# DLRM tower: the last shift's 39 field pairs as one matmul of rounded parts, and the diagonals on ScalarE

## The reference

```
for W in (f0, f1, f2):                       # f0 (39*39, 128); f1, f2 (128*39, 128)
    z = einsum('bfd,bgd->bfgd', x0, xk).reshape(b, f * g, d)
    cur = einsum('bpd,pm->bmd', z, W)        # 128 maps for each sample and each d
    outs.append(cur); xk = cur
z = sum over d of concatenate(outs, axis=1)  # (512, 384)
h = relu(concatenate([z, dense_ctx]) @ W_top1 + b_top1)
h = relu(h @ W_top2 + b_top2)
y = h @ W_top3
```

## Time and profile before

| what | value |
|---|---|
| median of 3 runs | 661.05 us (660.89 to 661.32) |
| profiled execution | 660.73 us, its span 658.5 us |
| busy in the span | PE 625.5, VectorE 522.7, GpSimd 502.3, ScalarE 341.3 us |
| mean granted TensorE clock | 0.99 |
| first strip matmul of chunk 0 | 42.41 us |
| first matmul of the dense layers that close the kernel (L893) | 628.47 us |

### The profile page before, as it was taken

The page is one execution under the profiler, slowest core; times in us unless marked ns, Lnnn a source line. Parts: engine busy times, 40 slices in busy tenths (PEclk is TensorE's granted clock), DMA queues, the critical chain, the costliest instruction groups (busy, mean ns, idle before and its releaser), DMA issues.

```text
span 658.5 us, 10966 instructions
## 1 busy us (share of the span) xinstructions
PE 625.5 (95%) x3110; PEld 470.4 (71%) x3110; DVE 522.7 (79%) x1655; ACT 341.3 (52%) x1152; POOL 502.3 (76%) x486
## 2 busy tenths in 40 slices
PE   0559999999999999999999999999999999999998
PEld 0237777777788777777788777777788777778873
DVE  4239988989985888989984888989984889988911
ACT  3224555646463565646463564646463564646612
POOL 6717888989894889989894888989894897657620
PEclk9969999999999999999999999999999999999999
DMA  7423405641320404031220404131230403000000
GB/s 226 106 57 111 127 3 134 236 105 32 68 68 2 132 3 121 15 90 47 60 75 3 131 4 110 25 92 44 52 84 2 131 4 104 27 1 2 0 1 0
DMA packets 59014, 43.40 MB, mean 66 GB/s; under 512 B 37648, under 2 KB 42926, under 8 KB 58826
## 3 DMA queue, kind: packets, MB, share of 16 engines
q1 hardware_dynamic: 52334, 37.52, 19.6%
q0 software_dynamic: 5120, 1.32, 2.9%
q10 hardware_dynamic: 1500, 3.87, 1.7%
HBM read 40.75 MB, written 1.94 MB: 65 GB/s over the span
## 4 chain that ended last, share of the span: by engine, by line
PE 91%; another core or an unknown queue 3%; DVE 2%; DMA 2%; ACT 1%; issue 1%; ACTq 1%; DVEq 0%
PE strip L816 22%; PE strip L820 22%; PE strip L817 22%; PE acc L776 14%; PE acc L847 4%; PE strip L834 3%; PE strip L847 1%; DVE scaled L593 1%; DMA g_sum<-in_L_rec_f 1%; PE strip L918 1%; PE acc L785 1%; ACT w_hi L717 1%; ACTq L720 1%; PE strip L896 0%
## 5 line engine op out<-in xcount | busy, mean ns | idle before, releaser
L593 DVE SCALAR_TENSOR_TENSOR scaled<-strip,x_t,scaled 128x128 f32<-128x128 f32 x1216 | 331.5, 340 | 31.0 <-PE strip L820 29.5
L816 PE MATMUL strip<-w_hi,x_hi 128*128 128x512 f32 (+1 forms) x640 | 297.0, 464 | 3.4 <-ACT x_hi L646 3.4
L820 PE MATMUL strip<-w_hi,x_lo 128*128 128x512 f32 (+1 forms) x640 | 249.4, 390 | 0.0
L817 PE MATMUL strip<-w_lo,x_hi 128*128 128x512 f32 (+1 forms) x640 | 248.8, 389 | 0.0
L488 POOL TENSOR_TENSOR added<-added,product 128x512 f32<-128x512 f32 x128 | 173.0, 1351 | 83.4 <-ACT product L702 76.9
L702 ACT ACTIVATE product<-strip,x_t 128x128 f32<-128x128 f32 x512 | 147.0, 373 | 126.5 <-PE strip L820 113.2
L478 POOL DMA_INDIRECT found<-in_tables,rows x160 | 159.6, 998 | 28.4 <-issue 11.2
L816 PEld LDWEIGHTS strip<-w_hi,x_hi 128*128 128x128 f32 x640 | 120.5, 188 | 52.5 <-issue 18.8
L817 PEld LDWEIGHTS strip<-w_lo,x_hi 128*128 128x128 f32 x640 | 120.8, 189 | 45.5 <-issue 25.3
L820 PEld LDWEIGHTS strip<-w_hi,x_lo 128*128 128x128 f32 x640 | 120.3, 188 | 25.8
L776 PE MATMUL acc<-z,w 117*128 117x512 f32 (+1 forms) x238 | 116.5, 572 | 9.1 <-issue 9.1
(11 more groups left out here) (57 smaller groups left out, 190.2 us busy)
## 6 DMA issues: line engine op xcount, KB each, us to landing
shifted<-x_fields SPq DMA_DIRECT2D x105, 234.0 KB
x_thrice<-x_fields SPq DMA_DIRECT2D x15, 234.0 KB
found<-in_tables,rows POOLq DMA_INDIRECT x160
w<-in_L_rec_f SPq DMA_DIRECT2D x1, 2496.0 KB, 11.9
g_sum<-in_L_rec_f ACTq DMA_DIRECT2D x4, 512.0 KB
shifted<-x_half_fields SPq DMA_DIRECT2D x10, 117.0 KB
x_once<-x_fields SPq DMA_DIRECT2D x15, 78.0 KB
x_fields<-found SPq DMA_DIRECT2D x15, 72.0 KB
```

What stands on the lines that cost most here:

```text
L593: dve.scalar_tensor_tensor(into, strip[:, slot_of_strip(q) % Y_BANKS, j, :], x0_t[:, c % 2, s, f:f + 1], onto, ALU.mult, ALU.add).then_inc ...
L816: pe.matmul(into, x1_hi[:, c % 2, columns], hi, start=True, stop=False)
L817: pe.matmul(into, x1_hi[:, c % 2, columns], lo, start=False, stop=False)
L820: pe.matmul(into, x1_lo[:, c % 2, columns], hi, start=False, stop=True).then_inc(strip_ready, 1)
```

## The change

For parts 3 to 16 (`STACKED_FROM = 3`) the seventh tile goes away. The pairs of shift 18 move into the eleven unused partitions (117 to 127) of tiles 2 to 5, in runs of eleven pairs, which need their own field ranges beside `x0_thrice` and `shifted` and, for tiles 4 and 5, a second copy `x0_thrice2`. The pairs of shift 19 are computed as a product `z0_last` in which each pair stands on three neighbouring rows. ScalarE rounds it to `z0_last_hi`; VectorE combines both with `roles` into `z0_stack`, whose three rows hold the rounded part, the rounded part and the rest (with a sign). The weights are made once in the same way (`w0_stack`: rounded, rest, rounded). One f32r matmul adds the three products to `acc0`. The products start at place 9 instead of 6, the matmuls at 15 instead of 12, the stacked one is at place 33. The diagonals are made by ScalarE in two activations with `mask` as the scale.

```
+STACKED_FROM = HALVES + 1
+FULL = T0 - 1
+EXTRA = P - ROWS
+EXTRA_FROM = FULL - 4
+EXTRA_PAIRS = [(EXTRA_FROM + k, k // 2 * EXTRA, k // 2 * EXTRA + (LAST_SHIFT - 1 if k % 2 == 0 else FIELDS - LAST_SHIFT + 1))
+               for k in range(4)]
-PRODUCT0_AT = [6, 9, 12, 15, 18, 21, 24]
-LAYER0_AT = [12, 15, 18, 21, 24, 27, 30]
+PRODUCT0_AT = [9, 12, 15, 18, 21, 24]
+LAYER0_AT = [15, 18, 21, 24, 27, 30, 33]
-PRODUCT0_LATE_AT = [10, 13, 16, 19, 22, 25, 28]
-LAYER0_LATE_AT = [16, 19, 22, 25, 28, 31, 34]
+PRODUCT0_LATE_AT = [11, 14, 17, 20, 23, 26]
+LAYER0_LATE_AT = [17, 20, 23, 26, 29, 32, 34]
+STACK_AT = (6, 17, 27)
+STACK_LATE_AT = (8, 18, 29)
+W0_STACK_AT = (1, 23)
...
+                at_least(sp, z0_last_ready, i - 1 - STACKED_FROM)
+                sp.dma_start(x0_thrice[0:ROWS, p, columns_of(i)], shifted_fields(i, 0, PER_TILE, 0)
                              ).then_inc(thrice_in[p], 16)
+                if i >= STACKED_FROM:
+                    sp.dma_start(x0_thrice[ROWS:P, p, :], some_fields(i, EXTRA_PAIRS[0][1])).then_inc(thrice_in[p], 16)
                 if i:
                     once(i)
+                if i >= STACKED_FROM:
+                    at_least(sp, z0_last_ready, i - STACKED_FROM)
+                    sp.dma_start(shifted_last[:], shifted_fields(i, LAST_SHIFT, PER_TILE, 0)
+                                 ).then_inc(shifted_last_in, 16)
+                for t in range(tiles_of(i) if i else T0_BY_SP):
+                    at_least(sp, z0_ready, pairs_before(i - 1) + t + 1 if i else 0)
+                    if i >= STACKED_FROM and t == EXTRA_PAIRS[2][0]:
+                        sp.dma_start(x0_thrice2[0:ROWS, p, :], shifted_fields(i, 0, PER_TILE, 0)
+                                     ).then_inc(thrice2_in[p], 16)
+                        sp.dma_start(x0_thrice2[ROWS:P, p, :], some_fields(i, EXTRA_PAIRS[2][1])
+                                     ).then_inc(thrice2_in[p], 16)
+                    if rows_of(i, t) == P:
+                        sp.dma_start(shifted[ROWS:P, t, :], some_fields(i, EXTRA_PAIRS[t - EXTRA_FROM][2])
+                                     ).then_inc(shifted_in[t], 16)
...
+            def products_last(i):
+                dve.wait_ge(thrice_in[p], 16 * (arrivals(i) + stacked_arrivals(i)))
+                dve.wait_ge(shifted_last_in, 16 * (k + 1))
+                at_least(dve, z0_stack_ready, k)
+                dve.tensor_tensor(z0_last[:], shifted_last[:], x0_thrice[0:ROWS, p, :], ALU.mult
+                                  ).then_inc(z0_last_ready, 1)
+            def stack(i):
+                dve.wait_ge(z0_last_ready, k + 1)
+                dve.wait_ge(z0_last_hi_ready, k + 1)
+                if k:
+                    dve.wait_ge(l0_step, T0 * i)
+                dve.scalar_tensor_tensor(z0_stack[:], z0_last[:], roles[:, 0:1], z0_last_hi[:].bitcast(F32),
+                                         ALU.mult, ALU.subtract).then_inc(z0_stack_ready, 1)
...
+            def high_last(i):
+                act.wait_ge(z0_last_ready, k + 1)
+                at_least(act, z0_stack_ready, k)
+                act.copy(z0_last_hi[:], z0_last[:]).then_inc(z0_last_hi_ready, 1)
+            def diagonal(c):
+                act.wait_ge(x0_t_ready, part_of(c, SUBS - 1) + 1)
+                act.wait_ge(mask_in, 16)
+                at_least(act, g_ready, c)
+                for b in range(TILE_B):
+                    last = act.activation(x0_diag[:, :, b, 0:FIELDS], x0_t[:, c % 2, :, :], ACT.Copy,
+                                          scale=mask[:, b:b + 1])
+                last.then_inc(diag_ready, 1)
...
+                if t == tiles_of(i):
+                    pe.wait_ge(z0_stack_ready, i - STACKED_FROM + 1)
+                    if i == STACKED_FROM:
+                        pe.wait_ge(w0_stack_ready, 1)
+                    pe.matmul(acc0[:], w0_stack[:], z0_stack[:], start=False, stop=True).then_inc(l0_step, 1)
+                    return
```

More of the change, by code:

```diff
@@ L71, in columns_of, with pairs_before, tiles_of, step_of_product @@
     return slice(HALF_N * i, HALF_N * i + HALF_N) if i < HALVES else slice(0, N)
+def pairs_before(i):
+    return T0 * min(i, STACKED_FROM) + FULL * max(i - STACKED_FROM, 0)
+def tiles_of(i):
+    return T0 if i < STACKED_FROM else FULL
+def step_of_product(m):
+    i = max(i for i in range(X0_PARTS) if pairs_before(i) <= m)
+    return T0 * i + m - pairs_before(i) + 1
+def rows_of(i, t):
+    return P if i >= STACKED_FROM and t >= EXTRA_FROM else ROWS
+def transfers_of(i, t):
+    return i + 1 + (max(i + 1 - STACKED_FROM, 0) if EXTRA_FROM <= t < FULL else 0)
+def stacked_arrivals(i):
+    return len(range(i, STACKED_FROM - 1, -2))
 def subs_of(i):
@@ L287, in build_program @@
         shifted_in = [sem(f"shifted_in_{t}") for t in range(T0)]
+        thrice2_in = [sem(f"thrice2_in_{k}") for k in range(2)]
+        shifted_last_in = sem("shifted_last_in")
+        w0_last_in = sem("w0_last_in")
+        roles_in = sem("roles_in")
+        w0_last_ready = sem("w0_last_ready")
+        w0_last_hi_ready = sem("w0_last_hi_ready")
+        w0_last_lo_ready = sem("w0_last_lo_ready")
+        w0_signed_ready = sem("w0_signed_ready")
+        w0_stack_ready = sem("w0_stack_ready")
+        z0_last_ready = sem("z0_last_ready")
+        z0_last_hi_ready = sem("z0_last_hi_ready")
+        z0_stack_ready = sem("z0_stack_ready")
         w0_ready = sem("w0_ready")
@@ L926, in _, with pair_rows @@
             last.then_inc(y_done, 1)
-def shift_rows():
-    upper = np.full((ROWS, T0), -1)
-    lower = np.full((ROWS, T0), -1)
+def pair_rows():
+    upper = np.full((P, T0), -1)
+    lower = np.full((P, T0), -1)
+    last_upper = np.full((ROWS, 1), -1)
+    last_lower = np.full((ROWS, 1), -1)
     for s in range(SHIFTS):
@@ L938, in shift_rows @@
                 lower[row, t] = h * FIELDS + g
-    return upper, lower
+    taken = set()
+    for t, begin, partner in EXTRA_PAIRS:
+        for k in range(EXTRA):
+            g, h = (begin + k) % FIELDS, (partner + k) % FIELDS
+            if frozenset((g, h)) not in taken:
+                taken.add(frozenset((g, h)))
+                upper[ROWS + k, t] = g * FIELDS + h
+                lower[ROWS + k, t] = h * FIELDS + g
+    assert taken == {frozenset((g, (g + LAST_SHIFT - 1) % FIELDS)) for g in range(FIELDS)}
+    for g in range(FIELDS):
+        h = (g + LAST_SHIFT) % FIELDS
+        last_upper[PER_TILE * g:PER_TILE * g + PER_TILE] = g * FIELDS + h
+        last_lower[PER_TILE * g:PER_TILE * g + PER_TILE] = h * FIELDS + g
+    return upper, lower, last_upper, last_lower
 def by_gathers(of_fields, at_once):
```

110 lines of the change are left out of this document (81 added, 29 removed).

## The result

The median went from 661.18 us (660.89 to 661.75, 4 runs) to 657.01 us (656.18 to 657.51, 4 runs): ratio 0.9934, 95% interval [0.9913, 0.9954]. So the change is faster, by 4.2 us or 0.7%, where 9.7 us were forecast (651.4, range 650.3 to 655.0). The profiled execution took 657.29 us, its span 655.7 (2.8 less than before).

A forecast was written before the change was run, and what follows sets the result against it. The prediction took PE's instruction stream to set the time from 42 us on. From 660.73 us, -8.8 (PE) and -0.9 (stall) gave 651.0, or 651.4 for the median; own range 650.4 to 653.6, widened to 650.3 to 655.0.

The forecast's parts named there:

- GpSimd paragraph: GpSimd does the same work, its waits for ScalarE shrink by 1.3 us in all, some 0.4 us stays; cost nothing.
- Eight such operations stay eight: VectorE's two-SBUF-operand operations, which don't overlap GpSimd additions, stay eight a chunk since the diagonal leaves.
- PE: In 14 stacked parts one f32 tile (0.86 us) gives way to one 0.233 us matmul: 8.8 us saved.
- upper bound of the matmul: Stacked matmul on PE: 0.44 us if its weight load stands in front (0.19 more), against 0.233 taken.
- The stall of the earlier trace: PE's late weight load for strip 7's bank: excess 1.5 us, all gone at most, none at least, 0.9 taken.
- VectorE: Stacking (0.89 us) replaces the diagonal (0.93): net nothing per chunk, bounds -0.25 to +1.2, covered by 2.12 us idle.
- the sign named: Sign of being right: VectorE's idle before strip 31 still above 1 us.
- weight operations of chunk 1: Once-only rounding of weights at place 23, about 1.3 us of VectorE, before its 2.12 us idle: nothing.
- ScalarE: Two diagonal activations and one rounding copy add 1.6 us a chunk and fit; nothing, at worst 0.5 us of VectorE's time.
- Transfers: About +19% bytes and added issues end some 5 us later, at the turn of the chunk; cost nothing.
- A: Rival: shifted GpSimd collisions, late banks at strips 10 to 14 or a showing load cost 0.2 to 0.5 us in 14 chunks: 654 to 658; chance 0.12.
- D: Rival: GpSimd holds the chunk at 35, needing 0.5 us more work to hold at 34.5, 1.1 for no gain; chance 0.02.

The follow-up runs named there:

- e1: Changed kernel with gathers (GpSimd's indirect field loads) moved out of ordinary chunks into chunk 0 and layer-2 chunks: 647.19 against 646.62 us for the kernel before, 1.001.
- e9: Changed kernel with no gather (GpSimd's indirect field load) in the last quarter of a chunk: 641.19 against 646.53 us for the kernel before, 0.9922.
- e2: Kernel before the change with the same dealing of gathers as e1: 656.75 us, 1.0164 of the kernel before.
- e10: Kernel before the change with the same dealing as e9, no gather in the last quarter of a chunk: 647.21 us, 1.0012 of the kernel before.
- e11: Kernel before the change with only the diagonals moved from VectorE to ScalarE: 647.14 us, 1.0005 of the kernel before.
- e14: Changed kernel as it is, the base on one chip with the early start: 640.07 us, 0.9887 of the kernel before.
- e16: e3 again, changed kernel without the stacking operation, on the same chip as e14: 638.81 us, 0.9877 of the kernel before.
- e3: Changed kernel with VectorE's stacking operation left out, the matmul reading z0_last_hi: 639.10 against 646.62 us for the kernel before, 0.9885.
- e12: Kernel before the change with tiles three places later and diagonals on ScalarE, all seven f32 tiles kept: 645.15 us, 0.9981 of the kernel before.
- e4: Kernel before the change with the seventh tile's matmul cut to 16 columns from part 3 on: 638.71 against 646.62 us, 0.9886.
- e17: Changed kernel with 22 gathers for 26 ahead of the loop and gathers dealt anew, ordinary chunks none in the last quarter: 649.25 against 660.74 us before, 0.9829.
- e7: Changed kernel with the diagonal back on VectorE as one operation at place 20: 669.41 against 661.29 us for the kernel before, 1.0112.
- e18: Changed kernel as it is, the base on the same chip as e17: 656.16 us, 0.9933 of the kernel before.
- e8: Kernel before the change with only its ordinary tile places moved three later: 665.21 us, 1.0058 of the kernel before.
- e13: As e9, changed kernel, with 22 gathers for 26 ahead of the loop and first chunks dealt anew: 638.36 against 646.95 us for the kernel before, 0.9868.

## Why the prediction was wrong

**Step that failed: the GpSimd paragraph.** "It does the same work", "it keeps some 0.4 us", "Cost: nothing". The same instructions took 32.6 to 33.1 us in the saturated chunks instead of 31.4. With gaps between instructions of 2.5 us that is 35.1, over the 34.32 that PE needs. Before, gaps and waits were 3.8 us, so 1.3 were waits. With those waits the 1.4 us that collisions with two-operand operations added a chunk cost nothing, and the prediction took the waits for free room and put no price on collisions on GpSimd's side. Chunks 1 to 14 gained 4.9 us of the forecast 9.7; the other 4.8 are lost here. It is shown by e1 and e9 (lighter or moved GpSimd work frees the chunks) with e2 and e10 as the control, and by PE's waits for L600.

**"Eight such operations stay eight"** was the count, and it misled. A collision is worth what stands on the other side: the diagonal left a place where it had cost GpSimd 0.1 us (e11), and the stacking came to one where it begins inside an addition and pushes the next gather (0.3 us; e14 to e16: 0.3 to 0.5 us in three of the four chunks). The larger part is not the stacking: e3, without it, still has GpSimd at 31.8 to 32.1. By the trace, the six products and the last one lengthen GpSimd's operations by 2.7 us in chunk 7, where seven products did so by 1.3 in chunk 6 before. What moved them against GpSimd's operations, the new places or PE's shorter chunk, no run separates; e12 has the places without the rise (30.9 to 31.5 us in the ordinary chunks 2 to 11), and e4 has the relief alone, with the rise in one chunk.

**PE: right.** Strips stand 0.93 us apart around place 33, the matmul costs 0.233. 34.94 (e12) to 34.32 is 0.62 us where 0.627 was forecast. Had all chunks run so, chunks 1 to 14 would take 11 x 34.32 + 3 x 43.01 = 506.6 and the time would be 5.0 less, of which 1.2 is chunk 2, 0.8 each of the other four saturated ones, 0.1 each of the layer-2 chunks and 0.2 chunk 6. The upper bound of the matmul, 0.44, would by its own terms be 0.233 + 0.19 = 0.42, and the range's lower end, 650.4, lacks the 0.3 us that the forecast adds for the median; neither bears on the miss.

**The stall of the earlier trace rows: right in effect, wrong in the reason.** Of the chunks that had it, 14 lost it (35.06 to 34.32) and 6 kept 0.17 of its 0.24 us; in the five saturated ones the wait for `x2_t` stands in its place. Where GpSimd's work is dealt out otherwise, it is gone from all (34.32 in e9 from chunk 3 on), so there the upper end, 1.5 us, held rather than 0.9. But e12 loses it without any PE relief, from places and diagonals alone; it does not need the 0.23 us behind strip 31.

**VectorE: too low a price, little harm.** The stacking took 1.12 us where 0.89 was taken, and the 91 products of 512 columns average 1045 ns, where 885 was read (the last product: 783). VectorE's work rose from 32.76 to 33.55 us in a saturated chunk, inside the bound of +1.2. Idle before strip 31 fell to 0.15 us in chunk 7, where over 1 was the sign named. It holds PE for 0.2 us between strips 20 and 21 of each saturated chunk, which is gone where GpSimd's work is lighter (e1, e9), and for over 1 us in chunk 2 of e9 and e17. There the weight operations of chunk 1, priced at nothing because an idle of 2.12 us would follow, found no such idle.

**ScalarE: right.** Two diagonals of 439 ns and a cast of 634: 1.5 us where 1.6 was forecast, and its work in a chunk rose by 1.1. That the move pays only together with the places was not in the prediction: e7 puts its absence at 12.7 us, e11 its presence alone at nothing.

**Start: the clock in chunk 0, the rest not settled.** The first strip was 1.0 us later and chunk 0 0.9 longer. The stretch of chunk 0 in the changed kernel had a mean granted clock of 0.93 of the higher level (2.4 GHz); before it was 0.96 over 39.02 us. PE had been idle for 3.4 us before its first strip in both.

```profile
43.43:83.38 39.95, 39.67 (x155) 30.08 (x156) 34.79 (x106) 19.41 (x67) 26.45 (x25) 0.93 0.40 118
```

Two strip intervals of chunk 0, the third and fourth, were 1.43 and 1.12 us, where before they were 0.96 and 0.70, and that is all of the 0.9: the lower level (1.2 GHz, strip matmuls 0.43 us apart) lasted until 48.8 us, before until 45.8. e18's chunk 0 is 38.76 and its first strip at 42.87, so a part of this varies between executions of one kernel. e8, a variant of the kernel before, had its first strip at 43.65, so the 1.0 us isn't shown to come from the change either.

**Transfers: right.** They don't hold the chunks, since e1 and e9 reach PE's 34.32 us with all of them.

**Rivals.** The time fell into A's 654 to 658. A's cause is right, that collisions with GpSimd's additions fall at other places, but not its path over late banks at strips 10 to 14. What holds the chunk is D's GpSimd, in five of eleven ordinary chunks, given 0.02 with "0.5 us more work a chunk to hold at 34.5 and 1.1 for no gain": the saturated chunks shown had 1.3 and 1.7 more and gained nothing. D was priced right and its chance was too low: GpSimd's work differs between chunks with the gathers (29.96 us with 9 in chunk 1, 33.06 with 11 in chunk 2) and with the collisions (31.01 in chunk 9, 32.63 in chunk 7, with 10 each).

## What to carry to other kernels

When the bound engine gets 2% faster, add up busy time and gaps of the next ones chunk by chunk, and ask which of their waits hid something else: GpSimd at 31.4 of 35.2 us looked free, and was the bound at 34.3. A VectorE operation with two SBUF operands is priced on both sides, since here it delayed and was delayed by the additions and gathers that GpSimd ran beside it. Then deal out the movable work of the new bound: another order of the gathers, of a kind that was worth nothing before the change (e10), raised its gain on one chip from 4.6 to 11.5 us, 4.4 of it by an earlier start and 2.1 by shorter chunks. On a chip with the early start e13 was 1.7 us below e14, with overlapping intervals.
